# Two-layer graph network: tail unrolled in a new order, neighbour sums transposed, edge tiles in contiguous halves, neighbours counted on VectorE

## The reference

```
# layer 1: masked attention with 8 heads of 16, then a feed-forward block
qkv = layer_norm(x, g1, be1) @ w_qkv
attn = softmax(where(adj != 0, q k^T / 4, -inf))
x = x + (attn @ v) @ w_proj + b_proj
x = x + gelu(layer_norm(x, g2, be2) @ w1 + b1) @ w2 + b2
# layer 2: one score per neighbour, the same mask
h = x @ Wt.T + bt                                   # 4096 x 64
s = leaky_relu(h @ Wa.T + ba, 0.2)                  # one score per row
w = softmax(where(adj > 0, s, -9e15), axis=1)
y = x + (w @ h) @ Wp.T + bp
out = gamma * (y - mean(y)) * rsqrt(var(y) + 1e-5) + beta
```

## Time and profile before

| | |
|---|---|
| median of 3 runs | 1380.0 us (1379.14 to 1380.53) |
| profiled execution | 1379.69 us |
| its span | 1377.9 us (1.8 us lie around it) |
| phases 1 and 2 | 0 to 1076 us |
| tail of layer 1 | 1076 to 1248 us |
| layer 2 | 1248 us to the end |

### The profile page before, as it was taken

One profiled execution on the slowest core, in us unless ns is written; L12 is line 12 of the kernel. 1 busy time (PEld: TensorE's weight loads), 2 busy tenths in 40 slices (PEclk: granted clock), 3 DMA queues, 4 the chain that ended last, 5 costly groups with the idle time before them and its releaser, 6 DMA issues.

```text
span 1377.9 us, 32788 instructions
## 1 busy us (share of the span) xinstructions
PE 1203.9 (87%) x12296; PEld 401.1 (29%) x12296; DVE 1138.8 (83%) x1599; ACT 1050.0 (76%) x1183; POOL 876.6 (64%) x913
## 2 busy tenths in 40 slices
PE   5547999999999999999999999999999277788994
PEld 3321111111111111111111111111111055567984
DVE  6656999999999999999999999999999145553544
ACT  4546999999999999999999999999999122220000
POOL 5675777777777777777777777777777022220323
PEclk9777999999999999999999999999999678899997
DMA  5002232332333233233224224323321831104992
GB/s 162 1 18 77 100 132 93 108 135 97 108 121 112 93 125 122 93 113 134 93 93 149 98 93 134 113 93 112 135 93 55 221 107 46 46 0 119 300 303 72
DMA packets 104276, 152.30 MB, mean 111 GB/s; under 512 B 4992, under 2 KB 84544, under 8 KB 95936
## 3 DMA queue, kind: packets, MB, share of 16 engines
q1 hardware_dynamic: 83456, 139.81, 31.1%
q10 hardware_dynamic: 20672, 10.49, 3.0%
HBM read 110.43 MB, written 39.85 MB: 109 GB/s over the span
## 4 chain that ended last, share of the span: by engine, by line
ACT 61%; issue 14%; DVE 9%; PE 7%; POOL 5%; ACTq 2%; POOLq 1%; DMA 0%; DVEq 0%; SPq 0%
ACT probs L1048 35%; ACT probs L1042 26%; POOL probs L948 2%; PE ps L469 2%; ACTq L277 1%; DVE probs L1151 1%; PE ps L1251 1%; POOL adj_in L580 1%; PE ps L1191 1%; DVE probs L1077 1%; DVE acc_sb L1159 1%; DVE v_sb L384 1%; PE ps L455 1%; DVE probs L1089 1%; POOL v_sb L250 1%
## 5 line engine op out<-in xcount | busy, mean ns | idle before, releaser
L1151 DVE SCALAR_TENSOR_TENSOR probs<-m,ps 128x512 f32<-128x512 bf16 (+1 forms) x1024 | 928.9, 951 | 33.2 <-PE ps L1251 15.0
L1048 ACT ACTIVATE probs<-probs 128x1536 f32<-128x1536 f32 x512 | 867.3, 1695 | 0.9
L984 POOL TENSOR_TENSOR probs<-probs,m 128x512 f32<-128x512 f32 x512 | 596.0, 1164 | 226.4 <-ACT probs L1042 197.2
L1264 PE MATMUL ps<-probs,v_sb 128*17 128x512 f32 x4096 | 539.2, 599 | 0.2 <-ACT probs L1048 0.2
L1251 PE MATMUL ps<-kq 32*128 32x512 bf16 x6144 | 426.3, 380 | 38.2 <-DVE probs L1151 9.7
L1042 ACT ACTIVATE probs<-ps 128x512 f32<-128x512 f32 x512 | 411.0, 803 | 23.4 <-PE ps L1251 22.7
L1251 PEld LDWEIGHTS ps<-kq 32*128 32x128 bf16 x6144 | 114.7, 93 | 565.3 <-ACT probs L1042 499.0
L963 POOL TENSOR_SCALAR m<-adj_in 128x512 bf16<-128x512 int32 x256 | 157.3, 615 | 4.0 <-issue 3.9
L1264 PEld LDWEIGHTS ps<-probs,v_sb 128*17 128x17 f32 x4096 | 68.2, 95 | 218.7 <-issue 210.2
L710 PE MATMUL ps<-probs,kq 128*128 128x193 bf16 x1024 | 88.8, 246 | 0.0
L710 PEld LDWEIGHTS ps<-probs,kq 128*128 128x128 bf16 x1024 | 86.0, 97 | 1.1 <-DMA kq<-mask_t 0.2
(11 more groups left out here) (126 smaller groups left out, 641.1 us busy)
## 6 DMA issues: line engine op xcount, KB each, us to landing
adj_in<-in_adj_t SPq DMA_DIRECT2D x64, 1024.0 KB, 5.6
mask_t<-m SPq DMA_DIRECT2D x64, 512.0 KB, 2.9
kq<-mask_t SPq DMA_DIRECT2D x12, 2048.0 KB, 17.3
kq<-mask_t ACTq DMA_DIRECT2D x4, 2048.0 KB, 17.3
attn_t<-acc_sb SPq DMA_DIRECT2D x16, 256.0 KB, 6.4
tail_words<-attn_t SPq DMA_DIRECT2D x8, 512.0 KB, 3.4
probs<-in_x SPq DMA_DIRECT2D x8, 256.0 KB, 4.2
tail_words<-in_x SPq DMA_DIRECT2D x8, 256.0 KB, 3.6
```

Of the source, the lines that this page charges most:

```text
L984: nc.gpsimd.tensor_tensor(pr, pr, m01[:, (k // 2) % MRING, :], ALU.mult).then_inc(postmasked, 1)
L1048: nc.scalar.activation(pr, pr, ACT.Exp, scale=UNIT).then_inc(exped, 1)
L1151: nc.vector.scalar_tensor_tensor(out=pr, in0=m.to_broadcast([P, n, CH]), scalar=1.0, in1=ps[:, b:b + n, :], op0=ALU.subtract, op1=ALU.add)\
L1264: last = nc.tensor.matmul(ps[RT * hh:RT * hh + VW, 6 + g, :], v_sb[:, t, h * VW:(h + 1) * VW], probs[:, k % SLOTS, hh // 2, (hh % 2) * CH: ...
```

## The change

The attention stays. From 1076 us on:

- **Start.** Weights come already laid out from the host (`wt_t`, `wp2`), so the two turned copies are gone. SyncE, not ScalarE, issues the mask loads, between its loads of the sums. `acc`, `xr` and `xb` have two buffers.
- **Steps.** The loops are written out. Step i on VectorE is now `hidden_low(i-2)`, `first_sum(i+1)`, `normalise_x1(i+1)`, `second_sum(i)`, `normalise_att(i+2)`, `hidden(i-1)`, `hidden_parts(i-1)`. The two copies of the split go to ScalarE (`hidden_high`, `hidden_middle`). The score comes out of the matmul `hidden`, as a 65th column, which leaves one instruction for it. `ff1` uses two banks in turn in place of four. GpSimd also adds up `h` over the chunks (`hidden_sum`), which replaces the 32 matmuls of L700.
- **No barrier** between tail and layer 2. TensorE begins the sums of chunk 0 before the last chunk's `hidden`.
- **Mask loads.** Halves are now 16 tiles with all 512 queries: one run of 16 KB per partition, in a ring of five halves.
- **Sums transposed.** `h3` is the stationary side, the mask the moving one with 512 columns: per tile one matmul of 128 columns of `h3` (high and middle part) and one of 64 columns (low part), which writes to partitions 0 to 63 or 64 to 127 in turn. That is 64 matmuls a chunk in place of 128. The turn through L720 is gone; the projection follows straight away, and the weights come after it.
- **Count.** The column of ones is gone. VectorE adds up the mask tiles in pairs (`degree`, two calls a chunk): instructions of 4096, 2048, 1024 and 512 bf16 elements per partition, and one more of 512 on the second call. Four matmuls of one column end the count.

```diff
-        edges = kq[:, 0:2 * NT * CH].rearrange("p (s t q) -> p s t q", s=2, t=NT)
+        edges = kq[:, :].rearrange("p (s t q) -> p s t q", s=5, t=NT // 2)
...
+        def load_edges(sp, n):
+            if n >= ERING:
+                sp.wait_ge(edges_used, n - ERING + 1)
+                sp.wait_ge(deg_step, 4 * (n - ERING) + 1)
+            j, half = n // 2, n % 2
+            sp.dma_start(edges[:, n % ERING, :, :], m_dram[j, :, half * HALF:(half + 1) * HALF, :])\
+                .then_inc(edges_in[n % ERING], 16)
...
         def tail_scalar(act):
-            for u in range(2):
-                for half in range(2):
-                    q = slice(half * CH // 2, (half + 1) * CH // 2)
-                    act.dma_start(edges[:, u, :, q], m_dram[u, :, :, q]).then_inc(edges_in[u][half], 16)
             act.wait_ge(tail_in, N_TAIL_IN)
-            act.wait_ge(wT_turned, 1)
-            nc.scalar.activation(wtT, ps[:, 0, 0:HID], ACT.Copy)
-            nc.scalar.activation(wpT[0:HID, :], ps[0:HID, 1, 0:D], ACT.Copy).then_inc(wT_copied, 1)
+            act.wait_ge(wa_made, 1)
+            nc.scalar.activation(wt_aug[:, HID:HID + 1], ps[:, B_HID, 0:1], ACT.Copy).then_inc(wa_copied, 1)
...
+            for i in range(NC):
+                if i >= 2:
+                    hidden_low(i - 2)
+                if i + 1 < NC:
+                    first_sum(i + 1)
+                    normalise_x1(i + 1)
+                second_sum(i)
+                if i + 2 < NC:
+                    normalise_att(i + 2)
+                if i >= 1:
+                    hidden(i - 1)
+                    hidden_parts(i - 1)
...
+            dve.wait_ge(csw_made, 1)
+
+            def degree(n):
+                j, half = n // 2, n % 2
+                e = edges[:, n % ERING, :, :]
...
+                nc.vector.tensor_tensor(wide, e[:, 0:8, :], e[:, 8:16, :], ALU.add).then_inc(deg_step, 1)
+                dve.wait_ge(deg_step, 4 * n + 1)
+                nc.vector.tensor_tensor(t8, wide[:, 0:4, :], wide[:, 4:8, :], ALU.add).then_inc(deg_step, 1)
+                dve.wait_ge(deg_step, 4 * n + 2)
+                nc.vector.tensor_tensor(t2, t8[:, 0:2, :], t8[:, 2:4, :], ALU.add).then_inc(deg_step, 1)
...
+            for j in range(NC):
+                add_parts(j)
+                if j + 1 < NC:
+                    degree(2 * j + 2)
+                weights(j)
+                residual(j)
+                if j + 1 < NC:
+                    degree(2 * j + 3)
+                finish(j)
...
+            def sums_high(n):
+                j, half = n // 2, n % 2
+                pe.wait_ge(edges_in[n % ERING], 16 * (n // ERING + 1))
+                if half == 0 and j >= 2:
+                    pe.wait_ge(s_made, j - 1)
+                for t in range(half * HALF, (half + 1) * HALF):
+                    nc.tensor.matmul(ps[:, BANK_A[j % 2], :], h3[:, t, 0:2 * HID], edges[:, n % ERING, t % HALF, :],
+                                     start=t == 0, stop=t == NT - 1)
+
+            def sums_low(n):
+                j, half = n // 2, n % 2
+                for t in range(half * HALF, (half + 1) * HALF):
+                    r = (t % 2) * HID
+                    last = nc.tensor.matmul(ps[r:r + HID, BANK_B[j % 2], :], h3[:, t, 2 * HID:3 * HID],
+                                            edges[:, n % ERING, t % HALF, :], start=t < 2, stop=t >= NT - 2)
+                last.then_inc(edges_used, 1)
...
+            pe.wait_ge(h_lo_made, NC // 2)
+            pe.wait_ge(gelu_made, NM * NC)
+            sums_high(0)
+            turn_x2(NC - 1)
+            sums_low(0)
             hidden(NC - 1)
...
+            pe.wait_ge(h_lo_made, NC)
+            sums_high(1)
+            sums_low(1)
+            column_sums()
+            for j in range(1, NC):
+                sums_high(2 * j)
+                sums_low(2 * j)
+                project_sums(j - 1)
+                sums_high(2 * j + 1)
+                sums_low(2 * j + 1)
+            project_sums(NC - 1)
```

More of the change, by code:

```diff
@@ L168, in gnn_kernel @@
[L168 to L178, removed]
@@ new lines, in finish @@
+            def finish(j):
+                dve.wait_ge(yr_step, 2 * j + 2)
+                for s in range(SUB):
+                    last = nc.vector.tensor_scalar(y[:, s, :], y[:, s, :], ymv[:, s, 0:1], yrs[:, s:s + 1],
+                                                   ALU.subtract, ALU.mult)
+                last.then_inc(y_normed, 1)
+            degree(0)
+            degree(1)
+            for j in range(NC):
+                add_parts(j)
[6 more added lines that the diff above has]
+                finish(j)
@@ L483, in hidden @@
                 for s in range(SUB):
[L484 to L485 removed]
+                    last = nc.tensor.matmul(ps[:, B_HID, s * (HID + 1):(s + 1) * (HID + 1)],
+                                            x2T[:, s * P:(s + 1) * P], wt_aug[:, 0:HID + 1], start=True, stop=True)
                 last.then_inc(hid_done, 1)
[L488 to L503 removed]
             turn_acc(0)
@@ new lines, in tail_tensor @@
+            turn_h2(0)
+            for i in range(NC):
+                ff1(i, (0, 1))
+                if i + 1 < NC:
+                    turn_att(i + 1)
+                ff1(i, (2, 3))
+                if i + 1 < NC:
+                    project(i + 1)
+                if i >= 1:
+                    turn_x2(i - 1)
+                ff2(i)
+                if i + 2 < NC:
+                    turn_acc(i + 2)
+                if i + 1 < NC:
+                    turn_h2(i + 1)
+                if i >= 1:
+                    hidden(i - 1)
@@ new lines, in column_sums @@
+            def column_sums():
+                pe.wait_ge(hsum_made, NC)
+                pe.wait_ge(x2_made, NC)
+                for s in range(SUB):
+                    last = nc.tensor.matmul(ps[0:HID, B_OUT, 0:P], hsum[:, s, :], onesf,
+                                            start=s == 0, stop=s == SUB - 1)
+                last.then_inc(cs_done, 1)
+                pe.wait_ge(cs_copied, 1)
+                nc.tensor.matmul(ps[:, B_OUT, P:2 * P], csT[0:HID, :], wp2_sb[0:HID, :], start=True, stop=True)\
+                    .then_inc(csw_done, 1)
```

674 lines of the change are left out of this document (332 added, 342 removed).

## The result

The changed kernel takes 1347.2 us (median of 4 runs, 1347.1 to 1348.5) against 1379.6 for the kernel before on the same chip: a ratio of 0.977, 95% interval 0.975 to 0.978, 32.4 us less. The prediction was 1366 (1342 to 1391): faster, as forecast, and inside the range, but by more than twice the 14 us forecast. The profiled execution has a span of 1345.4 us against 1377.9. So 2 us of a difference between two spans can come from there, and distances inside one trace are the safer measure.

What follows compares the result with a forecast made beforehand. Bounds before: ScalarE's mask issues at the start, VectorE's order in tail steps, TensorE in layer 2. Span: 1377.9 - 52.0 - 2.9 + 7 x (19.4 - 13.55) = 1364.0; forecast 1366 us, range 1342 to 1391.

Steps and rivals of the forecast that it cites:

- Start: Start of the tail: with SyncE issuing the mask loads, turn_acc(0) starts at about 1076.5 instead of 1097.3, 20.8 us gained.
- Steps: Tail steps: without hidden_parts ahead of normalise_att, later steps take 11.5 us instead of 18.3; ff1(7) at 1174.3.
- From `ff1(7)` to the first count: Tail end into layer 2: 9.3, 10.9 and 8.1 us, so both first degrees start at 1202.6.
- The count: VectorE in layer 2: bf16 pairs add at 0.54 ns a column, a degree costs 4.7 us, the second of a chunk 5.1.
- rival 1: VectorE's count: bf16 adds no faster than f32, 8.4 us more a chunk, 1433 us in all; chance 0.10.
- The chunk: Layer 2: VectorE becomes the bound with 16.4 us, plus 3.0 lost to GpSimd, 19.4 us a chunk.
- The root's two (1.2 us) fall into a `degree` and cost their length: Layer 2 chunk: GpSimd's two root instructions lengthen VectorE's additions by 1.2 us, part of GpSimd's 3.0.
- rival 2: Layer 2 chunk: GpSimd costs little, beside PSUM reads or waiting itself; 16.4 to 18 us a chunk, 1345 to 1356; chance 0.24.
- rival 3: Layer 2: TensorE becomes the bound again by its clock; at 1.2 GHz 23 us a chunk, 1391; chance 0.04.
- The end: From the last chunk's add_parts to the end of the span: 15.75 us instead of 18.65, 2.9 gained.

Runs made afterwards that it cites:

- Run 6: Kernel before, with SyncE instead of ScalarE issuing the four first mask loads, behind its loads of the sums: 1360.6 us, ratio 0.986.
- run 7: Kernel before, with only VectorE's normalise_att of chunk c+2 moved ahead of hidden_parts of chunk c-1: 1348.2 us, ratio 0.977.
- run 9: Changed kernel, with VectorE's normalise_att(i+2) put back behind hidden_parts(i-1) in the tail steps: 1355.2 us, ratio 0.982.
- run 3: Changed kernel, with the 32 low matmuls of each chunk done twice, the first time into unused banks: 1350.7 us, ratio 0.979.
- run 2: Changed kernel, with four more GpSimd power operations of 4 columns behind each chunk's beta, into an unread tile: 1350.2 us, ratio 0.979.
- run 1: Changed kernel, with GpSimd's gamma and beta operations touching one column of 128 instead of all: 1336.1 us, ratio 0.969.
- the shared count: Changed kernel, with half 0 of each chunk counted by VectorE and half 1 by TensorE: 1317.0 us, ratio 0.954.
- run 8: Kernel before, with first mask loads issued by SyncE and normalise_att moved ahead of hidden_parts, nothing else: 1328.1 us, ratio 0.963.
- run 11: Changed kernel, with the whole count on TensorE by 32-column ones blocks plus a ScalarE copy, VectorE's degree gone: 1323.0 us, ratio 0.959.

## Why the prediction was off, point by point

**Start** (20.8 us predicted, 21.7 measured). Right; 1.1 of the 21.7 is that phases 1 and 2 ended earlier in this execution. Run 6 shows the cause by itself.

**Steps** (11.5 predicted, 11.2 measured; `ff1(7)` at 1174.3 and 1171.3). The size was right. The cause that the prediction gave, VectorE's order, is shown to be enough (run 7), but it is not the only sufficient one (run 9): in the changed kernel the order is worth 1.3 us a step, not 7.

**From `ff1(7)` to the first count** (28.3 predicted, 27.9 measured; VectorE idle for 7.9, 10 predicted). A bf16 product of 512 columns over the full array took 0.22 us (16 in 3.63; 0.25 was taken), the 64-column ones 0.12 each (16 in 1.92): a pair takes the time of one, as assumed. That the whole stretch came out within 0.4 us is partly luck. The way to `h` took 0.7 us less up to the end of `ff2(7)` and 0.9 less from there, but half 1 and the column sums took 9.3 us instead of 8.1, because TensorE came out of its wait for `h` at the low clock (6 products in 2.60 us, 0.43 each; run 3). The prediction priced that clock as a rival in the chunks and for the last projection, not here.

**The count** (2.4 us for 4096 columns predicted, 2.29 measured; a `degree` 4.7, measured 4.65). The lower of the two bounds, 0.54 ns a column, held, and rival 1 falls. The Trainium skill, "VectorE: DVE Perf Modes", "The perf-mode tier table", gives 1224 ns for 2048 columns; the trace has 1.22 us.

**The chunk** (19.4 predicted, 17.25 on the mean of seven: 15.8 for the first, which has no gamma and beta beside it, then 17.47). This is the term that was mis-sized, and seven times 2.15 us are 15.1 of the 18.6 us between the 1364.0 forecast and the span of 1345.4. About 8 of the 15 are the root's two instructions, 4 are VectorE's own work, and 2 are gamma and beta, above all that the first chunk has none beside it. VectorE's own work was put at 16.4 and is 15.8; the row of instructions between 1209.28 and 1225.10 in the trace has degrees of 4.65 and 5.15, `weights` 2.05, `residual` 2.35, `finish` 1.0 and `add_parts` 0.6. The allowance of 0.2 for gaps was not needed, `residual` was 0.2 too long, and `finish` and `add_parts` 0.1 each. And **"The root's two (1.2 us) fall into a `degree` and cost their length"** is the step that failed. They cost nothing: VectorE's addition was under way each time, and the root waited for it. The second of them then worked on for 0.87 us after the addition of 2048 columns had ended at 1257.50, beside that of 1024 columns, which kept its 0.69; and four more such instructions a chunk cost nothing either (run 2). The other two were put at 0.5 and 1.27 and cost 0.7 and 0.96 (run 1). So GpSimd's price was 1.66, not 3.0; that is the mechanism of rival 2 (they "wait themselves"), with its numbers (16.4 to 18 us a chunk, 1345 to 1356), and the time lies there. The row behind the estimate, 1.10 us for an addition of 4 columns beside GpSimd, was of a wide GpSimd instruction that had started first; it was carried over to narrow ones that start second.

The Trainium skill, "SBUF — State Buffer", "SBUF: two separate sides", says that whoever starts first holds the pair of ports for the whole instruction. For gamma, beta and the root's first the trace agrees: L558 loses 0.7 to L345, which began 0.44 us earlier, L347 ends about one length of its work (1.13 of 1.27 us) after VectorE's instruction, and L337 as it does. For the root's second and for run 2 it does not: a GpSimd instruction of 4 columns that lasts 1.02 us ran beside a bf16 addition and neither was longer for it. The prediction took the rule's other case, GpSimd first, for all four.

**TensorE and its clock** (rival 3). The granted clock in a chunk is 0.84 to 0.90; after 5.6 us of waiting for VectorE, the projection's 8 matmuls took 2.05 us, against 1.14 in the shared count, where TensorE hardly rests (clock 1.00). This costs nothing in the chunks, as run 3 puts 3.8 us more on TensorE there without effect. Where TensorE's work lies in the open it does cost: the 1.2 us ahead of the first count, and 2.05 us instead of 1.14 for the last projection.

**The end**: 15.75 predicted, 15.4 measured. What is left of the difference is 3.1 us at the first `add_parts` (1212.4 against 1209.3). Of these, 3.0 stand already at `ff1(7)`: 1.6 at `ff1(0)`, of which 0.9 is the earlier start of the tail, and 1.4 from there on.

Left open: which of the tail's small parts (the halves of `ff1` in two banks, the 65th column) bring the 1 us between 12.2 and 11.2 a step was not tried.

## What to carry over

A change that is faster as a whole can hold a part that costs: here a moved call and a moved group of DMA issues in the old kernel bring 51 us (run 8), and in the changed one the count on the engine with room costs 24 (run 11). Before moving work to an engine with room, price it on both engines at the real rates (4.7 us against 1.05 for a half) and stop before it becomes the new bound: of the three splits of the count that were run, half on each engine was best. And where two engines slow each other, read from the rows which of them waits: here the wide GpSimd instructions made VectorE wait, the narrow ones waited themselves or ran beside it for nothing.

## What the chip showed that was not expected

- A GpSimd pow of 4 columns takes 1.02 us alone and 2.00 beside VectorE's additions, and these lose nothing; a multiplication of 512 f32 columns costs them 0.7, an addition 0.96.
- Products of 512 columns with 64 stationary columns in two alternating blocks took 0.12 us each, with 32 in four blocks 0.065 (16 in 1.05), against 0.22 for the full array: in these three widths, at the full clock, the time of one goes by its share of the array.
- 3.8 us more of products on TensorE made the first count only 1.8 us later, as the granted clock stayed at 1.00 after TensorE's next wait, where it was 0.53 without them (run 3).
- Four loads of 2 MB with runs of 512 bytes, issued one right behind the other, held ScalarE 0.67, 5.58, 7.17 and 7.17 us (the 20.68 of the earlier trace rows). SyncE's 16 issues of 2 MB with runs of 16 KB took 0.32 at the median and 1.40 at most, but they stood at least 3 us apart. Whether the long runs or the distance made them short was not told apart.
